# Edge list of a graph kernel: 117 columns permuted on TensorE through a ring of eight, 50 written by GpSimd at a pace, and four encoder banks

## What is computed

```
h    = sigmoid(layernorm(x) @ wenc.T + benc)          # 1250 x 500
h2   = h @ conv_weight
msgs = h2[src] * edge_weight                          # 21250 edges
agg  = segment_sum(msgs, dst)
hout = agg + h @ lin_weight.T
x    = x + hout @ wdec.T + bdec
```

## Time and profile before

| what | value |
|---|---|
| runs, median of 3 | 2487.7 us (2482.96 to 2495.9) |
| profiled execution: span from first to last instruction | 2611.6 us |
| profiled execution: time around the span | not listed |
| mean granted TensorE clock in the span | 0.956 |
| TensorE busy | 2363.0 us, 90% |
| VectorE busy | 1623.0 us, 62% |
| ScalarE busy | 993.7 us, 38% |
| GpSimd busy | 885.2 us, 34% |

### The profile page before, as it was taken

The page is one execution under the profiler, slowest core; times in us unless marked ns, Lnnn a source line. Parts: engine busy times, 40 slices in busy tenths (PEclk is TensorE's granted clock), DMA queues, the critical chain, the costliest instruction groups (busy, mean ns, idle before and its releaser), DMA issues.

```text
span 2611.6 us, 30845 instructions
## 1 busy us (share of the span) xinstructions
PE 2363.0 (90%) x10104; PEld 1779.6 (68%) x10104; DVE 1623.0 (62%) x2527; ACT 993.7 (38%) x1763; POOL 885.2 (34%) x843
## 2 busy tenths in 40 slices
PE   6578788897999979999999999999899898995998
PEld 3234233365787758877788888888777676874886
DVE  8243566756546447655455455457888889775665
ACT  4001122334334334312212212216788887544333
POOL 2651666600111215565520000014345563211543
PEclk9789899998999989999999999999999998997999
DMA  4002666623555447543533543537777786438884
GB/s 153 1 4 104 184 177 180 176 74 114 172 149 174 155 176 258 179 168 120 190 140 121 189 145 116 201 136 245 237 254 266 282 307 226 161 119 294 299 313 178
DMA packets 196050, 466.18 MB, mean 179 GB/s; under 512 B 29704, under 2 KB 30472, under 8 KB 195928
## 3 DMA queue, kind: packets, MB, share of 16 engines
q1 hardware_dynamic: 98248, 213.31, 23.5%
q0 software_dynamic: 64272, 190.20, 22.9%
q10 hardware_dynamic: 33408, 61.13, 6.2%
HBM read 364.20 MB, written 105.98 MB: 180 GB/s over the span
## 4 chain that ended last, share of the span: by engine, by line
PE 78%; DVE 9%; DMA 4%; issue 4%; another core or an unknown queue 3%; ACT 2%; DVEq 1%; POOL 0%; ACTq 0%; SPq 0%; POOLq 0%
PE pair L1377 8%; PE pair L1375 8%; PE pair L1376 8%; PE pair L1116 4%; PE pair L1393 3%; PE pair L1396 3%; PE pair L1413 2%; PE pair L1414 2%; PE pair L1415 2%; DVE U L2228 2%; PE pair L1098 2%; PE pair L1079 2%; PE pair L1261 2%; PE pair L1263 2%
## 5 line engine op out<-in xcount | busy, mean ns | idle before, releaser
L1554 ACT ACTIVATE sq_h<-quad 128x512 fp32r<-128x512 f32 x196 | 121.7, 632 | 461.7 <-PE pair L1377 411.3
L972 POOL DMA_INDIRECT rows_y<-y_rows,l_row x184 | 208.8, 1135 | 210.4 <-PE pair L1396 181.4
L1375 PE MATMUL pair<-sq_h,xh 128*128 128x512 f32 x700 | 273.6, 391 | 6.4 <-DVE sq_l L2549 4.6
L1376 PE MATMUL pair<-sq_h,xl 128*128 128x512 f32 x700 | 272.4, 389 | 0.0
L1377 PE MATMUL pair<-sq_l,xh 128*128 128x512 f32 x700 | 272.4, 389 | 0.0
L2637 DVE SCALAR_TENSOR_TENSOR low_y<-rows_y,l_inv,high_y 128x1024 fp32r<-128x1024 f32 x184 | 234.4, 1284 | 47.9 <-ACT high_y L1554 44.0
L914 POOL DMA_INDIRECT XT<-h_rows,l_src x184 | 177.5, 965 | 151.3 <-DMA h_rows<-OS 63.1
L1554 ACT ACTIVATE high_y<-rows_y,l_inv 128x1024 fp32r<-128x1024 f32 x184 | 210.5, 1144 | 41.7 <-PE pair L1396 26.5
L949 POOL DMA_INDIRECT inv_ring<-inv_count,at_ring x184 | 191.2, 1039 | 74.7 <-issue 56.2
L2549 DVE TENSOR_TENSOR sq_l<-quad,sq_h 128x512 fp32r<-128x512 f32 x196 | 131.1, 696 | 105.7 <-ACT sq_h L1554 83.8
L1116 PE MATMUL pair<-XT,XN 128*128 128x504 f32 x368 | 196.5, 669 | 0.0
(11 more groups left out here) (391 smaller groups left out, 5595.6 us busy)
## 6 DMA issues: line engine op xcount, KB each, us to landing
quad<-in_L_gnn_weight SPq DMA_DIRECT2D x28, 1024.0 KB
xh<-sum_parts SPq DMA_DIRECT2D x14, 1280.0 KB
xl<-sum_parts SPq DMA_DIRECT2D x14, 1280.0 KB
y_rows<-u ACTq DMA_DIRECT2D x70, 256.0 KB
tok_raw<-in_L_ffn_w SPq DMA_DIRECT2D x8, 2048.0 KB
tok_raw<-in_L_ffn_w SPq DMA_DIRECT2D x16, 1024.0 KB, 13.2
x_rows<-X SPq DMA_DIRECT2D x20, 512.0 KB, 6.4
pair<-pair_rows SPq DMA_DIRECT2D x18, 512.0 KB
```

The lines of the kernel that those rows point to most:

```text
L972: pool.indirect_dma_start(rows_y[s % RING1][:], None, y_rows, bass.IndirectOffsetOnAxis(ap=l_row8[:, s:s + 1], axis=0)).then_inc(y_in[s % ...
L1375: mm(o, high[:, k, :], sq_h[:, k, :], start=(k == 0), stop=False)
L1376: mm(o, low[:, k, :], sq_h[:, k, :], start=False, stop=False)
L1554: return nc.scalar.activation(dst, src, func, **kw)
```

## The change

The first 117 columns are permuted and 50 are scattered. The ring has eight buffers, cut out of the same `room`. GpSimd waits before each scatter from the fifth on, for two permuted columns more each time. The encoder's results go round four banks, and TensorE waits for the sigmoid of four results before; banks 2 and 3 hold the prefix sums of the sort at first, so before result 2 it also waits until VectorE has read those.

```diff
-SCATTERED = 100
+SCATTERED = 50
...
+PERM_RING = 8
...
-        perm_lane = room[:, :, 0:P]
-        perm_val = room[:, :, P:P + 2 * SLOTS]
+        perm_ring = room[:].rearrange("p a (b n) -> p (a b) n", n=HALF)
+        perm_lane = perm_ring[:, :, 0:P]
+        perm_val = perm_ring[:, :, P:P + 2 * SLOTS]
...
+        enc_bank = banks[0:4]
...
-                if written >= 8 and written % 4 == 0:
-                    pool.wait_ge(perm_ready, written // 2 - 3)
+                if written >= 4:
+                    pool.wait_ge(perm_ready, 2 * written - 6)
...
-                    permute(t, t % 4, first=(t == 0), final=(t == PERMUTED - 1))
+                    permute(t, t % PERM_RING, first=(t == 0), final=(t == PERMUTED - 1))
...
-                    if q >= 2:
-                        pe.wait_ge(a_read, q - 1)
+                    if q == 2:
+                        pe.wait_ge(v_read, V_PRE + 1)
+                    if q >= 4:
+                        pe.wait_ge(a_read, q - 3)
...
-                        last = mm(a_bank[q % 2][:, 0:n], w[:, k, c * P:(c + 1) * P], XT[:, k, lo:lo + n],
+                        last = mm(enc_bank[q % 4][:, 0:n], w[:, k, c * P:(c + 1) * P], XT[:, k, lo:lo + n],
...
-                    nc.scalar.activation(hT[:, c, lo:lo + n], a_bank[q % 2][:, 0:n], ACT.Sigmoid,
+                    nc.scalar.activation(hT[:, c, lo:lo + n], enc_bank[q % 4][:, 0:n], ACT.Sigmoid,
...
-                    dve.wait_ge(perm_done, t - 3)
+                    dve.wait_ge(perm_done, t - PERM_RING + 1)
...
-                permute(t, t % 4, first=(t < 4))
+                permute(t, t % PERM_RING, first=(t < PERM_RING))
```

## The result

The changed kernel takes 2518.9 us (median of four runs, 2515.4 to 2520.3) against 2488.7 for the kernel before (four runs, 2483.0 to 2495.9). The ratio is 1.0106, with a 95% interval of 1.0085 to 1.0127. The medians differ by 30.2 us; the ratio says 26 (21 to 32). The forecast was 2518, 30.3 above the median it started from. Single executions far off all others, one of 7148 us of the change and one of 4785 us of the kernel before (both in experiment 4), are left out of every median and ratio here.

A forecast was written before the change was run, and what follows sets the result against it. TensorE was taken to set the end: gathers start 3.5 us after h2. Fifty columns at 0.62 us add 31.0, the other parts nothing: 2487.7 + 31 = 2518.7, given as 2518, range 2510 to 2533.

The forecast's parts named there:

- the 67 us: Stall of 67.1 us in the profile before h2's end, with late reports from TensorE; assumed wholly absent from the runs.
- Fifty more columns on TensorE: Encoder and h2 stage: 117 permuted columns instead of 67 at 0.62 us, +31.0 us; h2 ends at 212.4 against 181.5.
- Fifty more columns on VectorE: Filling 117 columns at 1.01 us takes 118 us; VectorE stays ahead of TensorE, so nothing.
- Fifty scatters fewer: GpSimd: 50 x 1.26 = 63 us less work, which gives nothing since GpSimd was not the bound.
- The lower end of the range: If the list before came 9 us after h2 allows, the change gains these back: +22 us.
- The pace: GpSimd's wait before scatters: scatter 50 waits for 92 permuted columns, near 173 us; priced at nothing.
- The end of the list: VectorE's unpacking: list ready 0.8 us after h2, before the store frees the gathers at 3.5; nothing, 4 us if not.
- the banks, the ring: Four encoder banks and eight ring buffers: neither was short without late reports, so nothing.
- The one that takes the stall out of the runs: Rival, faster: runs hold the encoder-stage stall and the change removes it; gathers 36 us sooner, 2451; chance 0.19.
- the one that charges it to each scatter: Rival, no change: stall 0.67 us per scatter; 50 fewer save 33.6, columns cost 31.0, giving 2485; chance 0.11.
- The third: Rival: 50 scatters still stall a recorded execution; profile and runs both 31 us longer, 2518; 0.70 together with the forecast.
- The pair that the prediction named: Sign: recorded span shorter, near 2575, while runs get longer; would confirm the stall belongs to the recording.

The follow-up runs named there:

- experiment 4: The changed kernel, and the kernel before with only 50 scattered and 117 permuted columns, rerun on one chip: 2529.2 and 2528.2 us, each 1.0128 against the kernel before.
- experiment 1: The kernel before, unchanged, recorded again: 2495.2 us, ratio 0.9998 against the kernel before.
- experiment 3: The kernel before with 50 scattered and 117 permuted columns, its old ring of four, two banks and old pace: 2528.5 us, ratio 1.0134 against the kernel before.
- 2: Experiment 2: the changed kernel with 100 scatters and the old pace, leaving only banks, ring and new wait: 2496.2 us, ratio 0.9994 against the kernel before.
- experiment 7: The kernel before with 104 scattered and 63 permuted columns: 2493.4 us, ratio 0.9981 against the kernel before.
- 5: Experiment 5: the kernel before with 75 scattered and 92 permuted columns: 2510.0 us, ratio 1.0056 against the kernel before.
- 6: Experiment 6: the kernel before with 112 scattered and 55 permuted columns: 2503.1 us, ratio 1.003 against the kernel before.

## Why the prediction was right, point by point

**Are the 67 us in the runs? They are not, but the reason given was not borne out.** The one step on which the forecast turned holds: experiment 1 has neither the stall in the encoder nor the one in the segment sum. The prediction said that such reports "look like something the recording does". The recordings of nine executions speak against that: after the change and in the eight recordings of the experiments, the span is 1.8 to 1.9 us below the execution's own time, and neither the chain nor the waits name an unknown queue. What the profile of before holds belongs to that one execution; whether its being recorded had a part in it stays open. The prediction's argument from sizes pointed the right way, with 123.9 us between the span and the runs and too little idle time after 531 us to hold them, but it passed over the segment sum. Experiment 1's span is 118.6 us shorter than the one in the earlier trace rows: 64.4 of these lie before the end of h2, 38.7 in the segment sum, 15.3 behind it and 0.2 between.

The prediction set two pages against the trace, and the later recordings contradict neither. The Trainium skill, NOTIFIC — the notification-queue block, section 10 (Constraints, capacities, measured rates), says that writing an implicit notification record costs the engine no cycles. As far as the time of a whole execution can show it, the runs agree: experiment 1, recorded, took 2494.8 us among runs of 2485.2 to 2502.5. The Trainium skill, Runtime: NRT & Kernel Launch, section on the ~15µs preamble/postamble breakdown, gives a fixed gap of about 6.2 us by which a profile's total time exceeds the execution's. The span is not that total, and no run here shows the 6.2 us: in the nine later recordings the span is the shorter of the two, by 1.8 to 1.9 us. The 123.9 us were a difference between two executions, and the prediction took them for a case of this rule.

**Fifty more columns on TensorE: right, +31.0 predicted.** The record of the changed kernel has h2's end at 211.75 for 212.4, experiment 3 against 2 has 30.3 us, and the runs of the change have 26 us (21 to 32) over the kernel before at first and 32 (24 to 39) in experiment 4. That the median came out within 1 us of 2518 is luck beside spreads of this size. The pieces of the earlier trace rows, counted, were enough to rebuild a stage that the profile of before didn't show undisturbed: experiment 1 lies at 181.4 (184.18 less the slow start's 2.8) for 181.5.

One term of the new sum is gone in the changed kernel: the pause of 0.6 us before h2, where by the code TensorE waits for ScalarE's last sigmoid. With 67 columns or fewer it is there (0.61 in experiment 7, as in the earlier trace rows); after the change a column stands there, and h2 follows it without a pause. From TensorE's timeline after:

```profile
153.51 0.78 PE L1060 MATMUL pair<-room 128*128 128x368 f32 x2
154.28 1.10 PE L1103 MATMUL pair<-W,U 128*128 128x512 f32 x2
```

Without that term the prediction's stage is 164.7 us and h2 ends at 211.8, for 211.75 measured. So a column costs the 0.62 us that were predicted, and 50 of them 31.0 less 0.6.

**Fifty more columns on VectorE: right.** It still finishes the last of them ahead of TensorE: in the changed kernel it waits 10.7 us for TensorE before it unpacks.

**Fifty scatters fewer: right, nothing.** The list of before was ready at 180.96 (predicted near 182) and the gathers were let go at 187.69 by h2's store. The lower end of the range, a list that came 9 us later than h2 allows, was not so; experiment 7 shows that from 104 scatters on the list is the later one.

**The pace: right in price, wrong in place.** The last scatter starts at 161.85, not near 173. The semaphore counts columns that VectorE has filled, and with eight buffers VectorE runs ahead; the prediction allowed for that and gave the later time. It changes nothing, as experiment 4 shows.

**The end of the list, the banks, the ring: right.** The list is ready 0.85 us after h2 (0.8 predicted); experiment 2 prices banks, ring and the new wait together at a ratio of 0.9994.

**The rivals.** The one that takes the stall out of the runs (2451) and the one that charges it to each scatter (2485) fall with experiment 1: the runs have no stall to give. The third, that the change relieves nothing even in a recorded execution, can't be put to the test, since the stall has not come back.

**What the profile would show.** The pair that the prediction named, a shorter recorded span and longer runs, is what came. Its size was off: 2575 was expected and 2513.6 was recorded, because the prediction looked for late reports in the encoder alone, while the segment sum was 37.4 us and what follows it 23.6 us longer in that execution. And the pair did not confirm what the prediction wanted it to. It shows only that the two recorded executions differ; that the runs of before are without the stall was shown by recording them again.

**Two slips, without effect on the forecast.** 2518.7 rounds to 2519, not to 2518. And of the weakest slices in the earlier trace rows one, with 5 tenths, is not among the first nine but the thirty-seventh.

## What to carry to other kernels

Set a profile's span against the runs before you read it: if it is longer than all of them, here by 5%, then its stalls are first of all a property of that execution, and the same work rebuilt from its pieces (so many matmuls by the time of one) tells how the stage runs without them. Work moved from an idle engine to the one that sets the end costs its full time there, however much it relieves the other: here 50 columns at 0.62 us, and the 63 us taken from GpSimd returned nothing. Where two engines share one job, the best share is where both end together, and one recording on each side brackets that point; here it lay between 100 and 104 of 167 columns.

## What the runs showed that was not expected

**One execution with late reports.** In the profile of before, VectorE, ScalarE and GpSimd sit in waits put down to "remote" in the stage of the scatters and in the segment sum. By the code the columns of the ring, the sigmoid and the gathers wait there for TensorE, and the one case that the prediction worked out was 31.6 us late. GpSimd issues indirect transfers in both stages; it does so later too, where only 3.8 us of such waits are listed. The waits of before, over the whole span, name them (in total, times, longest; the lines of the encoder's sigmoid, VectorE's columns and the gathers):

```profile
ACT U L1599 <- remote: 61.2, 2, 38.4
DVE room L2178 <- remote: 52.8, 8, 15.0
...
POOL XT L914 <- remote: 9.4, 4, 3.9
```

None of the nine later recordings has such a row. What disturbed that execution stays open; no experiment could bring it back.

**Two starts.** Before the encoder, the eight transposes of a tile take 1.94 us at first and about 1.07 later, with a granted clock listed as 1.00 all along. Where the change from one to the other falls differs between executions, whatever the kernel. From the timeline of TensorE, the fourth tile of transposes after the change:

```profile
26.59 1.07 PE L1037 MATMUL pair<-ident,XN 128*128 128x128 f32 x8 [0.42 <-ACT XT L1559]
```

and in experiment 1, with the encoder's first result behind it:

```profile
26.59 1.94 PE L1034 MATMUL pair<-ident,XN 128*128 128x128 f32 x8 [0.35 <-ACT XT L1554]
29.31 9.10 PE L1079 MATMUL pair<-XT,W 128*128 128x512 f32 x16 [0.78 <-ACT XT L1554]
```

The same 16 matmuls took 7.11 us after the change. The recordings of experiments 1, 2, 3 and 5 have the late form, and everything on TensorE after it, h2's end included, comes about 3 us later; those of experiments 6 and 7 lie between, 0.5 to 0.6 us behind the early form. A difference of 3 us between two single recordings of this kernel therefore says nothing, and differences of h2's end are best taken between two recordings with the same start, as 30.3 us above.

**A granted clock of 1.00 beside matmuls at two speeds** is the part of this that the rows don't explain: the level listed is that of 2.4 GHz, and the longer transposes take 1.8 times as long as the shorter (1.94 / 1.07).
